# A fused attention and mixture-of-experts layer on one core: the normaliser of linear attention in four column groups, its chain and its spread moved

## The reference, cut to what matters

```
xn  = layernorm(x)
out = x + attention(xn) + ffn(xn)

attention:  q, k = elu(xn @ Wq + bq) + 1, elu(xn @ Wk + bk) + 1   (16 heads of 16)
            v = xn @ Wv + bv
            kv = einsum('bkhd,bkhm->bhdm', k, v)
            out = einsum('bqhd,bhdm->bqhm', q, kv)
            normalizer = max(einsum('bqhd,bkhd->bqh', q, k), 1e-6)
            (out / normalizer) @ Wo + bo

ffn:        swiglu(xn @ w_in.T) @ w_out.T                          (shared layer)
            + sum over the 2 chosen experts of 8: weight * swiglu(xn @ w1.T) @ w2[e].T
```

## Time and profile before

| what | value |
|---|---|
| median of 3 timed runs | 1070.78 us (1067.65 to 1071.2) |
| profiled execution, its own time | 1058.75 us |
| its span, first to last instruction | 1056.8 us |
| TensorE busy | 1012.4 us, 96% of the span |
| VectorE / ScalarE / GpSimd busy | 672.9 / 398.8 / 491.5 us |
| mean granted TensorE clock | 0.995 |
| first stage, about | 11 to 610 us |

### The profile page before, as it was taken

One profiled execution on the slowest core, in us unless ns is written; L12 is line 12 of the kernel. 1 busy time (PEld: TensorE's weight loads), 2 busy tenths in 40 slices (PEclk: granted clock), 3 DMA queues, 4 the chain that ended last, 5 costly groups with the idle time before them and its releaser, 6 DMA issues.

```text
span 1056.8 us, 21589 instructions
## 1 busy us (share of the span) xinstructions
PE 1012.4 (96%) x6662; PEld 910.4 (86%) x6663; DVE 672.9 (64%) x1681; ACT 398.8 (38%) x676; POOL 491.5 (47%) x489
## 2 busy tenths in 40 slices
PE   5999999999999999999999889999999999999996
PEld 5889879888888888898888779999999999999996
DVE  7887797788779778877977634444443444444343
ACT  3454354345445444544444322222222222222221
POOL 5343343534343443334344445555555555555534
PEclk9999999999999999999999899999999999999999
DMA  8012111201211120211111032222222122222321
GB/s 269 24 53 73 52 40 52 72 20 57 68 52 40 52 72 26 64 54 52 40 52 53 12 82 71 64 72 61 69 69 71 63 69 69 63 68 69 65 45 21
DMA packets 55585, 64.55 MB, mean 61 GB/s; under 512 B 18829, under 2 KB 45581, under 8 KB 55568
## 3 DMA queue, kind: packets, MB, share of 16 engines
q1 hardware_dynamic: 42624, 35.86, 11.3%
q0 software_dynamic: 12944, 28.47, 9.9%
HBM read 37.16 MB, written 28.58 MB: 62 GB/s over the span
## 4 chain that ended last, share of the span: by engine, by line
PE 60%; DVE 22%; issue 12%; ACT 3%; DMA 1%; POOL 1%; SPq 0%; DVEq 0%; ACTq 0%; POOLq 0%
PE bank L309 19%; PE bank L310 19%; PE bank L311 18%; DVE xn L715 4%; PE bank L381 3%; DVE stats L701 2%; DVE gated L795 1%; DVE lmax L726 1%; DVE phiq L825 1%; DVE phik L808 1%; PE bank L502 1%; ACT expt L617 1%; ACT expt L619 1%; ACT gated L598 1%; DVE rn L857 1%
## 5 line engine op out<-in xcount | busy, mean ns | idle before, releaser
L598 ACT ACTIVATE gated<-bank 128x512 f32<-128x512 f32 (+1 forms) x140 | 83.0, 593 | 264.2 <-PE bank L311 224.6
L309 PE MATMUL bank<-wexp_hi,h_hi 128*128 x600 | 170.2, 284 | 0.3 <-DVE h_lo L961 0.3
L310 PE MATMUL bank<-wexp_lo,h_hi 128*128 x600 | 168.5, 281 | 0.0
L311 PE MATMUL bank<-wexp_hi,h_lo 128*128 x600 | 168.5, 281 | 0.0
L997 POOL TENSOR_TENSOR h_lo<-gated,h_hi 128x512 fp32r<-128x512 f32 x64 | 83.8, 1309 | 170.5 <-ACT h_hi L602 169.0
L602 ACT CAST h_hi<-gated 128x512 fp32r<-128x512 f32 (+1 forms) x140 | 86.4, 617 | 159.1 <-DVE gated L795 158.4
L795 DVE TENSOR_TENSOR gated<-gated,bank 128x512 f32<-128x512 f32 (+1 forms) x140 | 95.2, 680 | 77.5 <-ACT gated L598 77.5
L971 DVE SCALAR_TENSOR_TENSOR res<-bank,cur,res 128x256 f32<-128x256 f32 x150 | 62.2, 477 | 123.1 <-PE bank L311 120.7
L1058 POOL DMA_INDIRECT out<-res,idx_cur x75 | 74.2, 989 | 102.9 <-DVE res L971 88.9
L309 PE MATMUL bank<-xnT_hi,wexp_hi 128*128 128x512 f32 (+1 forms) x304 | 117.7, 387 | 1.0 <-DVE xnT_lo L952 1.0
L310 PE MATMUL bank<-xnT_lo,wexp_hi 128*128 128x512 f32 (+1 forms) x304 | 117.7, 387 | 0.0
(11 more groups left out here) (171 smaller groups left out, 2506.6 us busy)
## 6 DMA issues: line engine op xcount, KB each, us to landing
xt<-x SPq DMA_DIRECT2D x16, 512.0 KB, 3.6
xn_d<-xn SPq DMA_DIRECT2D x16, 512.0 KB, 2.9
base_d<-res SPq DMA_DIRECT2D x16, 512.0 KB, 4.5
wstage<-w_exp SPq DMA_DIRECT2D x16, 320.0 KB, 4.2
tab_d<-wexp_hi SPq DMA_DIRECT2D x12, 128.0 KB, 5.5
phik<-tab_d SPq DMA_DIRECT2D x76, 2.0 KB
xn<-xn_d,idx_next POOLq DMA_INDIRECT x76, 2.8
res<-base_d,idx_cur POOLq DMA_INDIRECT x76
```

The source lines that it names most:

```text
L309: e.matmul(to, w_hi, m_hi_, start=first_, stop=False, skip_group_check=free)
L310: e.matmul(to, w_hi, m_lo_, start=False, stop=False, skip_group_check=free)
L311: return e.matmul(to, w_lo, m_hi_, start=False, stop=last_, skip_group_check=free)
L598: act.activation(gated[:, j % 2, 0:cols], bank[gate_bank][:, 0:cols], ACT.Silu).then_inc(sil, 1)
```

## The change

The normaliser's matmul is turned round: khead (now 32 columns, each head twice) is the stationary operand and the queries' feature map the moving one. The tiles of tokens go to four groups of 32 output rows of bank 6, so that the result is already heads x tokens, 128 x 128. The transposes of rn, ScalarE's copy to `rsplit` and their semaphore go. VectorE's chain works on 128 x 128 in five steps: maximum, reciprocal, high part, a step that leaves the high part in the even 16 rows and (negated difference) the low part in the odd 16 rows of each group, and a product with a mask that lays the four groups out on a diagonal of 512 columns (`rdiag`), which the spread reads with 128 rows.

The chain moves from ahead of gate 2 to behind gate 2, the rank addition and `normalise(b + 1)`; the rank addition now stands ahead of `normalise(b + 1)`. The spread moves on TensorE from ahead of y to the middle of the part of h 0 to 2, behind tiles 0 and 1; its second matmul writes bank 4 instead of bank 6, and so waits for the low part of m. Behind tiles 2 and 3 comes the part of h 3, and the part of qn and m is now last. In the last batch the copy of the tile list (L868) comes behind the chain. The constants grow by 37 columns.

```diff
-        spread = sb("spread", [32, DC, P], f32r)
+        spread = sb("spread", [P, DC, P], f32r)
-        khead = sb("khead", [P, DC, 16], f32)
+        khead = sb("khead", [P, DC, 32], f32)
-        rn = sb("rn", [P, TB, 32], f32)
+        rn = relut[:, 0, DC * P:(DC + 1) * P]
+        rhigh = relut[:, 0, (DC + 1) * P:(DC + 2) * P]
+        rdiag = qn_hi[:, 1, :].rearrange("p (t n) -> p t n", t=TB)
...
-                for t in range(TB):
-                    for c in range(DC):
-                        mm = pe.matmul(bank[6][:, 16 * t:16 * t + 16], phiq[:, c, t * P:(t + 1) * P], khead[:, c, :],
+                for c in range(DC):
+                    for t in range(TB):
+                        mm = pe.matmul(bank[6][32 * t:32 * t + 32, 0:P], khead[:, c, :], phiq[:, c, t * P:(t + 1) * P],
                                        start=(c == 0), stop=(c == DC - 1))
...
-                pe.wait_ge(rn_rdy, b + 1)
-                for t in range(TB):
-                    mm = pe.transpose(bank[7][0:32, t * P:(t + 1) * P], rn[:, t, :], ident)
-                mm.then_inc(nb_done, 1)
...
-                pe.wait_ge(rhi_rdy, b + 1)
-                for c in range(DC):
-                    mm = pe.matmul(bank[6 + c][:, :], spread[:, c, :], rsplit, start=True, stop=True)
-                    mm.then_inc(nb_done, 1)
...
+                pe.wait_ge(rank_rd, b + 1)
+                pe.wait_ge(hlo_rdy, HC * b + 3)
+                y_shared(0)
+                y_shared(1)
+
+                pe.wait_ge(rn_rdy, b + 1)
                 pe.wait_ge(mlo_rdy, b + 1)
+                for c in range(DC):
+                    mm = pe.matmul(bank[7 - 3 * c][:, :], spread[:, c, :], qn_hi[:, 1, :],
+                                   start=True, stop=True)
+                    mm.then_inc(nb_done, 1)
+                y_shared(2)
+                y_shared(3)
+                pe.wait_ge(hlo_rdy, HC * (b + 1))
+                for t in range(TB):
+                    mm3(pe, y(t), h_hi[:, 3, t * P:(t + 1) * P], h_lo[:, 3, t * P:(t + 1) * P],
+                        wout_hi[:, 3, :], wout_lo[:, 3, :], False, False, True)
                 pe.wait_ge(qlo_rdy, DC * (b + 1))
                 for t in range(TB):
                     for c in range(DC):
...
-                        act.wait_ge(nb_done, 4 * b + 2)
-                        act.copy(rsplit, bank[7][0:32, :]).then_inc(rhi_rdy, 1)
...
-                dve.wait_ge(nb_done, 4 * b + 1)
-                whole, high_part = rn[:, :, 16:32], rn[:, :, 0:16]
-                dve.tensor_scalar(whole, bank[6][:, 0:64].rearrange("p (t h) -> p t h", t=TB), EPS_N, None, ALU.max).then_inc(kstep, 1)
-                dve.wait_ge(kstep, 6 * b + 4)
-                dve.reciprocal(whole, whole).then_inc(kstep, 1)
-                dve.wait_ge(kstep, 6 * b + 5)
-                dve.tensor_copy(high_part.bitcast(f32r), whole).then_inc(kstep, 1)
-                dve.wait_ge(kstep, 6 * b + 6)
-                dve.tensor_tensor(whole, whole, high_part, ALU.subtract).then_inc(rn_rdy, 1)
                 gate(2, HC * b + 2, 4, sil_rdy, gate_rdy)
                 if not last:
+                    ranks_in(b)
                     normalise(b + 1)
-                    ranks_in(b)
-                else:
+                dve.wait_ge(nb_done, 3 * b + 1)
+                dve.tensor_scalar(rn, bank[6][:, 0:P], EPS_N, None, ALU.max).then_inc(kstep, 1)
+                dve.wait_ge(kstep, KS * b + 4)
+                dve.reciprocal(rn, rn).then_inc(kstep, 1)
+                dve.wait_ge(kstep, KS * b + 5)
+                dve.tensor_copy(rhigh.bitcast(f32r), rn).then_inc(kstep, 1)
+                dve.wait_ge(kstep, KS * b + 6)
+                dve.scalar_tensor_tensor(rn, rhigh, low_row, rn, ALU.mult, ALU.add).then_inc(kstep, 1)
+                dve.wait_ge(kstep, KS * b + 7)
+                dve.tensor_tensor(rdiag, rn.unsqueeze(1).broadcast_to([P, TB, P]),
+                                  own_block.unsqueeze(2).broadcast_to([P, TB, P]), ALU.mult).then_inc(rn_rdy, 1)
+                if last:
                     dve.wait_ge(info_done, 1)
...
-                    dve.wait_ge(nb_done, 4 * b + 3 + c)
-                    dve.tensor_tensor(qn[:, c, :], phiq[:, c, :], bank[6 + c][:, :], ALU.mult).then_inc(qn_rdy, 1)
+                    dve.wait_ge(nb_done, 3 * b + 2 + c)
+                    dve.tensor_tensor(qn[:, c, :], phiq[:, c, :], bank[7 - 3 * c][:, :], ALU.mult).then_inc(qn_rdy, 1)
```

More of the change, by code:

```diff
@@ L39, in layer_program @@
     UNIT = (2 * 1024 + E * HC * D) // B
+    KS = 7
     EPS_LN, EPS_N = 1e-5, 1e-6
@@ L82, in layer_program @@
         m_hi, m_lo = pair("m", [P, DC, D])
-        rsplit = qn_hi[0:32, 1, :]
         NROW = 16 + 4 * NSLOT
-        stay = sb("stay", [P, 2 * P + DC * 16 + NROW + 6], f32)
+        stay = sb("stay", [P, 2 * P + DC * 32 + NROW + 11], f32)
         ident = stay[:, 0:P]
         head = stay[:, P:2 * P]
-        heads = stay[:, 2 * P:2 * P + DC * 16].rearrange("p (c n) -> p c n", c=DC)
-        crow = stay[:, 2 * P + DC * 16:2 * P + DC * 16 + NROW]
-        cpart = stay[:, 2 * P + DC * 16 + NROW:]
+        heads = stay[:, 2 * P:2 * P + DC * 32].rearrange("p (c n) -> p c n", c=DC)
+        crow = stay[:, 2 * P + DC * 32:2 * P + DC * 32 + NROW]
+        cpart = stay[:, 2 * P + DC * 32 + NROW:]
         triones = sb("triones", [P, 2, P], bf16)
@@ L158, in layer_program @@
         tok0 = cpart[:, 2:6]
+        low_row = cpart[:, 6:7]
+        own_block = cpart[:, 7:11]
         bank = [ctx.enter_context(nc.psum_tensor(f"bank{i}", [P, 512], f32)) for i in range(8)]
@@ L204, in layer_program @@
         hhi_rdy = sem("hhi_rdy")
-        rhi_rdy = sem("rhi_rdy")
         qhi_rdy = sem("qhi_rdy")
@@ L498, in batch, with y_shared @@
                     transposes((2, 3), t_done, (kvT_rdy, sil_rdy), (b + 1, HC * b + 3), xn_rdy, b + 2)
-                pe.wait_ge(rhi_rdy, b + 1)
-                for c in range(DC):
-                    mm = pe.matmul(bank[6 + c][:, :], spread[:, c, :], rsplit, start=True, stop=True)
-                    mm.then_inc(nb_done, 1)
                 def y(t):
                     return bank[5 + t // 2][:, (t % 2) * D:(t % 2 + 1) * D]
[L508 to L512, removed]
+                def y_shared(t):
                     for j in range(HC - 1):
@@ L519, in batch @@
                     for c in range(DC):
[L520 to L525, removed]
+                        mm = mm3(pe, y(t), qn_hi[:, c, t * P:(t + 1) * P], qn_lo[:, c, t * P:(t + 1) * P],
+                                 m_hi[:, c, :], m_lo[:, c, :], False, c == DC - 1, True)
                     if t % 2 == 1:
@@ L823, in batch @@
                     dve.wait_ge(eq_rdy, DC * b + o + 1)
-                    wait(dve, nb_done, 4 * (b - 1) + 1)
+                    wait(dve, nb_done, 3 * (b - 1) + 1)
                     dve.tensor_tensor(phiq[:, o, :], expt[:, o, :], relut[:, o, :], ALU.add).then_inc(phiq_rdy, 1)
@@ L831, in batch @@
                 dve.tensor_copy(ksum[:, :], acc[:, :, P]).then_inc(kstep, 1)
-                dve.wait_ge(kstep, 6 * b + 1)
+                dve.wait_ge(kstep, KS * b + 1)
                 for c in range(DC):
@@ L1095, in constants @@
     heads = (f == np.arange(16)[None, None, :]).astype(np.float32)
-    spread = np.ascontiguousarray(np.concatenate([heads, heads], 2).transpose(2, 1, 0))
+    heads = np.concatenate([heads, heads], 2)
+    spread = np.ascontiguousarray(np.tile(heads.transpose(2, 1, 0), (4, 1, 1)))
     pairs = [(g, j, i) for g in range(2) for j in range(4) for i in range(4) if j < i]
@@ L1105, in constants @@
     crow = np.broadcast_to(crow, (P, crow.size))
-    part = np.stack([p * P, p] + [t * P + p for t in range(4)], 1)
+    part = np.stack([p * P, p] + [t * P + p for t in range(4)] + [-(p // 16 % 2)] + [p // 32 == t for t in range(4)], 1)
     stay = np.concatenate([ident, head, heads.reshape(P, -1), crow, part], 1)
-    pad = np.zeros((P - 32, 2 * P))
-    other = np.concatenate([tri, np.concatenate([spread.reshape(32, -1), pad])], 1)
+    other = np.concatenate([tri, spread.reshape(P, -1)], 1)
     return {"c_stay": stay.astype(np.float32), "c_round": other.astype(np.float32)}
```

6 lines of the change are left out of this document (3 added, 3 removed).

## The result

The changed kernel took 1078.0 us (median of 7 timed executions, 1075.3 to 1081.8) beside 1067.9 for the kernel before (7, 1065.3 to 1071.2): a ratio of 1.0091 [1.0065, 1.0117], 0.9% slower. Timed again on another chip it was 1.0081 [1.0057, 1.0105]. The forecast was 1067.5 us and 0.3% faster. The time lies inside the range given (1061 to 1083 us), on the side of a rival that had 18%.

A forecast was written before the change was run, and what follows sets the result against it. VectorE with ScalarE and GpSimd bounds each batch up to T, the next input's first transpose, TensorE after. 0.41 - 0.1 - 0.09 = 0.2 us over 15 batches, 3.3 in total with the last batch, gave 1067.5 us; range 1061 to 1083.

The forecast's parts named there:

- What sets T: First transpose of the next normalised input: xn, held by GpSimd's two low parts, sets it; unchanged within 0.1 us.
- xn gets the port first: Rival, 20%: xn takes the shared port before GpSimd's low part; 0.33 us more saved for 14 batches, 1063.
- The normaliser: Its matmuls ahead of T, 1.86 us: nothing saved up to 1.3 us saved by four groups at once; 0 for the time.
- The clock falls: Rival, 18%, slower: the wider hole ahead of T halves TensorE's clock; two batches give 1074, five 1084, ten 1101.
- The price of a fall: Half-clock stretch where TensorE bounds: costs about half its length, 3.4 us of 6.7.
- The spread: Spread matmuls behind T, now 128 rows between halves of y: cost 0.45 us, 0.41 saved a batch, lower bound 0.
- The new wait: TensorE at the spread, for rn and m_lo: about 0.1 us, bounds 0 and 0.4; rival of a long wait 12%.
- The last batch: End of first stage: y ends some 0.3 us earlier; info copy 1.2 us later, hidden by the second group's gather.
- The shift by 12 us: Whole kernel: the timed median lies 12 us above the profiled execution, so 1055.4 is moved to 1067.5.

The follow-up runs named there:

- fill of 3: The changed kernel with three unused 512 column matmuls a batch ahead of the transposes of xn: 1068.3 us, 1.0004 of the kernel before.
- all holes filled: Changed kernel, info copy ahead of the chain, unused matmuls before xn's transposes (eight), info transposes (twelve) and stage 2's first transposes (eight): 1064.1 us, 0.9958 of the kernel before.

## Why the prediction was wrong, step by step

- **What sets T: right.** T less the batch's start is 26.33 for 26.51 us in the one profile and 26.71 in the second of the change. These differ by more than the 0.1 us named, but to both sides, and the four profiles of the kernel before lie at 26.39 to 26.58: no shift one way. The first xn takes 1.19 us (1.2 forecast), the second 1.35, the last two 0.40. GpSimd kept both turns; the rival in which xn gets the port first fell.
- **The normaliser: at its upper bound.** 1.86 to 0.65 us. The Trainium skill, page "TensorEngine Tiling (Array Packing)", section "Theoretical Speedup", gives up to four times for 32 columns. Before, the 16 records started 0.11 us apart; now four start together every 0.09 to 0.11 us, so this trace agrees.
- **The step that failed** is the one that followed: "0 for the time, and the wait of 0.85 in batch 5 grows to 1.3 to 2.6 us". It grew to 2.1. The price was not 0 but about 13 us. The rival *The clock falls* had place and cause right; that ten falls came, one of the three numbers that it priced, is luck. It got 18% against one argument, "holes of 1.6 us, four of them, brought none". Four holes in one execution are weak evidence: in three more executions of the same kernel four of eight such holes (1.53 to 1.56 us) brought a fall. The upper bound of the groups should have carried most of the chance, and with it the fall.
- **The price of a fall: too high.** 3.4 us were forecast, half of a stretch of 6.7 us. The stretches in the loop are half as long, 3.41 us. In them the matmuls of y start 0.213 us apart instead of 0.118, not twice that, which makes 3.41 x (1 - 0.118 / 0.213) = 1.5 us. In the kernel before 1.50 was measured. In the change 0.28 of it takes the place of the wait at the spread (next point), which leaves 1.2 to 1.3. Ten falls were put at 1101; at the measured price they are 1067.5 + 13 = 1080. The Trainium skill's page "TensorE: Matmul & The Clock Gate", section "HAM oscillation — how this bites in real kernels", tells of a wait that sends the engine to half clock in every turn of a loop. This trace agrees in kind, with ten turns of fifteen.
- **The spread: mis-sized.** 0.41 less 0.1 of wait less 0.09 was forecast. The 0.09 stand ahead of T, so that by its own terms 0.31 belongs to the part behind T (it named 10.1 for 10.33); measured there are 0.12 (10.21 for 10.33) in every batch without a fall. TensorE's timeline in batch 3 of the profile after, from the last matmul of y's first half on:

```profile
157.03 0.28 PE L312 MATMUL bank<-wout_hi,h_lo 128*128 128x256 f32 x1
157.33 0.71 PE L512 MATMUL bank<-qn_hi,spread 128*128 128x512 f32 x2
157.88 0.28 PE L310 MATMUL bank<-wout_hi,h_hi 128*128 128x256 f32 x1
```

  The two matmuls take 0.55 in the stream (0.45 forecast), and they start 0.30 behind the last of y where 0.12 is the spacing: a wait of 0.18 for m_lo. In batch 5, where TensorE comes later because of the fall, the same place reads

```profile
231.62 0.28 PE L312 MATMUL bank<-wout_hi,h_lo 128*128 128x256 f32 x1
231.74 0.62 PE L512 MATMUL bank<-qn_hi,spread 128*128 128x512 f32 x2
232.19 0.28 PE L310 MATMUL bank<-wout_hi,h_hi 128*128 128x256 f32 x1
```

  with 0.12 and 0.45 us. So the price of 0.45 was right for a stream that does not stop, and it is the wait that was mis-sized: it costs 0.18 and 0.10 more behind it, 0.28 us for the 0.1 forecast. The new wait was not long; that rival fell too. 15 batches: 1.8 us for 3.0.
- **The last batch: wrong.** "1.2 us later, but TensorE waits anyway". The copy came 3.1 us later, for the chain met a low part of GpSimd, and TensorE's first wait in the second stage is for a gather whose table loads wait for this very copy (`infoi_rdy`), where the forecast looked at the second group's gather: the first transposes came 3.7 us later, up to 4 us of time.
- **The shift by 12 us: right in kind.** The profiled execution of the kernel before was a short one. Its other profiles are 2 to 5 us longer, 1.5 to 3 of them falls.

The sum, in place of the old: ten falls a profile, one of them double in the second, +13 to +14; the falls that the kernel before has itself, -2 to -3 (five in four profiles, but its timed executions have the mean clock of the profiles with two); the info copy, 0 to +4; the spread, -1.8. That is 8 to 14 us, and 8.7 to 10.1 were timed. How much of the copy's price counts in the change itself stays open. Open is also why the timed executions of the kernel before (medians 1066 to 1070) lie above its four profiled ones (1058.8 to 1063.6) by more than their falls; three of those are from a chip where its one timed execution took 1062.3, so part of it may be the chip.

## What to carry to other kernels

A wait that costs nothing can still hold up the clock. Where an edit takes TensorE work from ahead of a wait that recurs in a loop, read how long TensorE will idle there, compare it with holes whose clock several executions have shown, and put other work into the hole in the same edit, even useless work. And ask of each "it waits anyway" what that wait hangs on.

## What the runs showed of the hardware

- How the granted clock went with the hole ahead of T: 0.6 to 1.1 us brought no fall in four profiles of one kernel, 1.3 to 1.57 five in fifteen, 1.66 nine in fourteen, and 1.9 to 2.7 ten in fifteen and ten in fourteen in the two profiles of the change. Beside the fill of 3, 1.4 brought none in twelve and about 2.0 one in three, so that the length of the hole alone does not tell. Which batches fall differs from execution to execution.
- Adding 26 us of matmuls that nobody reads (eight a batch) made the kernel 12 to 13 us shorter.
- At a granted clock of 0.50 the matmuls of y started 0.213 us apart, at 1.00 0.118: 1.8 times and not twice.
- A stretch of 3.41 us at 0.50 cost 1.50 us where TensorE set the time, 1.3 where it also took up a wait, and nothing in batch 2 of the second profile of the change, where VectorE set the time.
- The mean clock of an execution is no measure of its time by itself (0.991 to 0.995 with all holes filled, with the time the same). Over executions of the kernel before, 0.001 of mean clock went with 1.1 us on one chip (35 executions, correlation -0.78), 0.9 on a second (35, -0.75) and 0.5 on a third (19, -0.56).
- Four column groups of 32 output rows ran fully at once, 16 records of 128 columns in 0.65 us.
